# A ViT block with windowed attention and a top-2 expert layer: VectorE splits the first half, the second half's output product moves behind the first expert unit

## The reference

```python
h = tok(x)                      # patch embedding, layer norm, FFN, 8-head attention, FFN
h = layernorm(h + attn(h))      # one attention over the 64 tokens of an image
# ffn(h):
x = x + attention(rmsnorm(x)) @ wo.T            # 4 heads, causal
flat = rmsnorm(x) * ln2_w
probs = softmax(flat @ router_w.T)              # 8 experts
weights = top2(probs), divided by their sum
out = sum_e weights[:, e] * ((silu(flat @ w1[e].T) * (flat @ w3[e].T)) @ w2[e].T)
h = layernorm(h + x + out)
```

## Time and profile before

| | us |
|---|---|
| median of three runs (126.09 to 126.19) | 126.18 |
| the profiled execution | 125.92 |
| its span, first to last instruction | 124.1 |
| PE busy | 111.9 (90%) |
| DVE busy | 84.9 (68%) |
| ACT busy | 62.7 (50%) |
| POOL busy | 15.5 (12%) |

### The profile page before, as it was taken

How to read it: one execution, slowest core, us unless ns; L and a number is a source line. 1 busy time by engine, 2 the same in 40 slices (tenths; PEclk the granted TensorE clock), 3 DMA queues, 4 the chain that set the end, 5 groups by cost and what they waited for, 6 DMA issues and landing times.

```text
span 124.1 us, 2332 instructions
## 1 busy us (share of the span) xinstructions
PE 111.9 (90%) x904; PEld 75.4 (61%) x910; DVE 84.9 (68%) x183; ACT 62.7 (50%) x123; POOL 15.5 (12%) x42
## 2 busy tenths in 40 slices
PE   5998978899999889998699998899999999989950
PEld 2345637486777655775587895787888873325540
DVE  0003325797999496579797653489689978999951
ACT  4005367956323185654764638475475656245240
POOL 7400035000000000000022004090012230000000
PEclk9999999999999999999999999999999999999996
DMA  4999980000000000000000000000000000000003
GB/s 132 392 404 428 416 352 5 0 0 0 5 0 0 0 8 0 3 0 5 0 0 0 5 0 0 0 5 0 0 0 0 0 0 3 0 0 5 0 0 85
DMA packets 2682, 6.99 MB, mean 56 GB/s; under 512 B 1264, under 2 KB 1392, under 8 KB 2544
## 3 DMA queue, kind: packets, MB, share of 16 engines
q1 hardware_dynamic: 2128, 6.72, 13.9%
q10 hardware_dynamic: 544, 0.13, 0.5%
HBM read 6.59 MB, written 0.26 MB: 55 GB/s over the span
## 4 chain that ended last, share of the span: by engine, by line
PE 67%; DVE 19%; ACT 5%; issue 4%; POOL 2%; POOLq 1%; DVEq 0%; ACTq 0%
PE PS L650 7%; PE PS L651 7%; PE PS L292 4%; PE PS L317 3%; PE PS L533 3%; PE PS L327 3%; PE PS L658 3%; PE PS L284 3%; PE PS L519 3%; PE PS L381 3%; DVE top L1136 2%; DVE shifted L1138 2%; PE PS L391 2%; PE PS L667 2%; PE PS L356 2%
## 5 line engine op out<-in xcount | busy, mean ns | idle before, releaser
L650 PE MATMUL PS<-xf,up_hi 128*128 128x512 f32 x44 | 17.8, 404 | 0.0
L651 PE MATMUL PS<-xf,up_lo 128*128 128x512 f32 x44 | 17.4, 395 | 0.0
L1330 DVE TENSOR_TENSOR shared_h<-PS,shared_f 128x512 f32<-128x512 f32 x22 | 14.9, 683 | 3.2 <-ACT shared_f L921 2.7
L921 ACT ACTIVATE shared_f<-PS 128x512 f32<-128x512 f32 x22 | 13.0, 596 | 6.3 <-PE PS L651 6.3
L1136 DVE TENSOR_REDUCE top<-PS 128x8 f32<-128x512 f32 x12 | 8.3, 688 | 3.7 <-PE PS L356 1.8
L650 PEld LDWEIGHTS PS<-xf,up_hi 128*128 128x128 f32 x44 | 8.3, 188 | 2.1 <-DVE shared_h L1330 0.2
L749 ACT ACT_TABLE_LOAD x7 | 9.0, 1283 | 0.8 <-PEq L1537 0.7
L651 PEld LDWEIGHTS PS<-xf,up_lo 128*128 128x128 f32 x44 | 8.3, 188 | 1.8
L820 ACT ACTIVATE probs<-PS 128x512 f32<-128x512 f32 x8 | 4.8, 597 | 7.9 <-PE PS L367 7.8
L1138 DVE TENSOR_TENSOR shifted<-PS,top 128x512 f32<-128x512 f32 x12 | 8.3, 692 | 0.4
L1066 DVE TENSOR_REDUCE sq_sums<-squares 128x4 f32<-128x256 f32 x8 | 3.3, 418 | 7.3 <-ACT squares L772 4.2
(11 more groups left out here) (196 smaller groups left out, 213.8 us busy)
## 6 DMA issues: line engine op xcount, KB each, us to landing
shared_x<-x_dram SPq DMA_DIRECT2D x3, 576.0 KB, 4.6
shared_x<-x_dram SPq DMA_DIRECT2D x3, 512.0 KB, 7.8
up_w<-pack_d_dram SPq DMA_DIRECT2D x1, 1408.0 KB, 12.1
pack_c_sb<-pack_c_dram SPq DMA_DIRECT2D x1, 796.5 KB, 13.5
pack_b_sb<-pack_b_dram SPq DMA_DIRECT2D x1, 455.0 KB, 9.2
down_w<-pack_e_dram SPq DMA_DIRECT2D x1, 352.0 KB, 13.7
pack_a_sb<-pack_a_dram SPq DMA_DIRECT2D x1, 162.0 KB, 6.3
out_dram<-normed SPq DMA_DIRECT2D x2, 64.0 KB, 1.8
```

What stands on the lines that cost most here:

```text
L650: mm(up, up_hi[:, at:at + P], moving, start=True, stop=False)
L651: mm(up, up_lo[:, at:at + P], moving, start=False, stop=True).then_inc(sem("up_mm"), 1)
L921: f(gate[:, n % UPBUF, :], PS[:, UP_BANKS[n % UPBUF][0], :], ACT.Silu).then_inc(sem("gated"), 1)
L1330: v.tensor_tensor(hh[:, ch, :, g * HC:(g + 1) * HC], PS[:, UP_BANKS[n % UPBUF][1], :].rearrange("q (s c) -> q s c", s=2), gate[:, n % UPBU ...
```

## The change

`PARTS_AT` goes from 5 to 6 and `ROUTE_AT` from 6 to 7. The high part is made by VectorE and not by ScalarE, in both halves. For half 0 VectorE does high and low part ahead of the second half's `divide`, and TensorE turns the parts ahead of `mixed_to_features("att3", 7, 1)`. `output3(1)` goes from before unit 0 to between units 0 and 1, with `squares3(1)` behind ScalarE's first Silu. VectorE's `sum_squares("rms2", 1)` goes behind its product of unit 1, `normalised(1)` and `high_part(1)` behind unit 2, and `low_part(1)` and `residual(1)` behind unit 3. One more idle matmul is in `stay_awake`.

```diff
-        HIGH_AFTER = 1
-        PARTS_AT = 5
-        ROUTE_AT = 6
+        PARTS_AT = 6
+        ROUTE_AT = 7
...
 (TensorE)
-            stay_awake(2, 1)
+            stay_awake(3, 1)
+            parts_to_features(0)
             mixed_to_features("att3", 7, 1)
-            parts_to_features(0)
-            output3(1)
...
             for n in range(2 * CH):
                 g, ch = n // CH, n % CH
+                if n == 1:
+                    output3(1)
...
 (ScalarE)
-            def high_part(g):
-                act.wait_ge(sem("rms2_normed"), g + 1)
-                f(parts[:, 4 * g:4 * g + 4, 0, :].bitcast(F32R), tiles(h5n)[:, 4 * g:4 * g + 4], ACT.Copy)\
-                    .then_inc(sem("high_ready"), 1)
...
             bring_table(ACT.Silu)
-            high_part(0)
+            turned_copy(0)
             attended_copy3(1)
-            turned_copy(0)
-            squares3(1)
...
-                if n == HIGH_AFTER:
-                    high_part(1)
+                if n == 0:
+                    squares3(1)
...
 (VectorE)
+            def high_part(g):
+                ts = slice(4 * g, 4 * g + 4)
+                ve.wait_ge(sem("rms2_normed"), g + 1)
+                v.tensor_copy(parts[:, ts, 0, :].bitcast(F32R), tiles(h5n)[:, ts]).then_inc(sem("high_ready"), 1)
...
             normalised(0)
+            high_part(0)
+            low_part(0)
             divide("att3", 7, 1, FH, FHD)
-            low_part(0)
             turned_copy(0)
-            sum_squares("rms2", 1)
             residual(0)
...
-                if n == HIGH_AFTER - 1:
+                if n == 1:
+                    sum_squares("rms2", 1)
+                if n == 2:
                     normalised(1)
-                if n == HIGH_AFTER:
+                    high_part(1)
+                if n == 3:
                     low_part(1)
                     residual(1)
```

## The result

The changed kernel takes 128.69 us (median of four, 128.13 to 128.81) against 126.14 for the kernel before (126.04 to 126.19): a ratio of 1.0196, interval 1.017 to 1.0221. It is slower by 2.55 us; 129.1 was forecast, within 128.1 to 129.9. In experiment 1 the slower three of six executions are in the median but not in the ratio, which leaves out what lies more than 1.5% above a kernel's fastest execution; in every other kernel here nothing had to be left out.

What follows compares the result with a forecast made beforehand. TensorE, with 67% of the chain of waits, was taken as the bound in the units, VectorE after them. Parts of -0.42, +0.55, +1.73, +0.93, -0.06 and +0.24 summed to 2.97 us more: 129.1 us, range 128.1 to 129.9.

Steps and rivals of the forecast that it cites:

- Into unit 0: Ahead of unit 0: VectorE's 0.29 copy and earlier parts let unit 0 start at 79.36, 0.42 us gained.
- The output product behind unit 0: Between units 0 and 1: `output3(1)` adds 0.55 us, and `sum_squares(1)` starts at 82.86, before at 80.31.
- The copy beside the casts: Second half's high part on VectorE: one GpSimd cast holds it until 85.36; it ends at 85.65, `residual(1)` at 87.30.
- Rivals A and B: Second half's high part: A, casts don't hold the copy, 128.6, chance 0.17; B, both casts hold it, 129.7, chance 0.12.
- The group of transposes: TensorE behind unit 5: transposes load at 87.36 and unit 6 starts 0.55 us later, at 87.91.
- The router a unit later: Router's chain one unit later while `ROUTE_TURN` stays 20: TensorE waits some 1.3 at the turn; 0.93 us in the sum.
- The constant of 13.50: From the unit's start behind the router's products to `routes_to_rows`: 13.50 us, putting the turn at 103.23.
- Both stalls: TensorE waits 1.86 us ahead of the transposes and some 1.3 ahead of `routes_to_rows`, the second on top.
- Centring: After the units: second centring moves ahead of the first `weight_rest`, pushes VectorE by 0.33, of which 0.24 us is left.
- Rivals C and D: C: one stall only (transposes or turn), 127.3 or 127.8, chance 0.10; D: side chains keep up with TensorE, 125.6, chance 0.05.
- Rival E, the clock: In the units: TensorE's clock falls to 1.2 GHz for two units after the new stalls, 131.0, chance 0.06.

Runs made afterwards that it cites:

- experiment 1: Changed kernel with `PARTS_AT` back to 5 and `ROUTE_AT` back to 6: 130.59 us, ratio 1.0287 to the kernel before.
- experiment 3: Changed kernel with the second half's VectorE steps each one unit earlier: 127.42 us, ratio 1.0139 to the kernel before.
- experiment 4: GpSimd's casts `pick_rest` and `pick` put ahead of the second norm's roots: changed kernel 128.33 us, ratio 1.0192; kernel before, ratio 0.9981.
- experiment 2: Changed kernel with `PARTS_AT` 5, `ROUTE_AT` 6 and seven idle matmuls ahead of TensorE's wait for `residual(1)`: 128.34 us, ratio 1.0187 to the kernel before.
- experiment 5: Changed kernel with `routes_to_rows` ahead of unit 21 instead of 20: 127.59 us, ratio 1.0143 to the kernel before.
- experiment 6: Changed kernel with the residual's sums back behind units 17 and 18, centrings behind 19 and 20: 127.85 us, ratio 1.0161 to the kernel before.
- all four repairs: Changed kernel with second half's VectorE steps one unit earlier, GpSimd's casts early, sums and centrings at old units, `routes_to_rows` ahead of unit 21: 125.96 us, ratio 1.0011.

## Why the prediction was right, and where its sum was off

The mechanism came as forecast, in this order of steps:

- **Into unit 0.** Forecast at 2.49, measured 2.51. The 0.29 for the copy, estimated between rows of other operations, held exactly; its bounds were 0.28 and 0.42, so some luck is in that.
- **The output product behind unit 0.** `sum_squares(1)` forecast at 5.99, measured 5.89. Going from 3.44 to 5.89 is the root of the loss, and experiment 3 gives 1.07 of it back by one unit.
- **The copy beside the casts.** It was held by one cast: 0.43 (forecast 0.46). Rivals A and B, no cast and both, are out by experiment 4. The term that was mis-sized is the next: I had `pick` start only when the copy was done, at 0.91 behind T. It started 0.69 behind `normalised(1)`, as in the earlier trace rows, and only ran 1.10 instead of 1.04. So the low part, 0.65, was held for 0.24 and not for 0.39, and the residual ended at 10.15 and not at 10.43: 0.28 too much, 0.10 of it already in the place of `sum_squares`.
- **The group of transposes.** I gave it 0.55 before the next unit's load; after a pause it takes 0.39 (86.54 to 86.93). 0.16 too much. With this the turn is 2.29 later, not 2.73.
- **The router a unit later.** The distance from the router to the turn is 13.48 to 13.52 in every row of the table with the clock up but one (13.88, where the casts are early and unit 20 stands in front of the turn, so that TensorE itself is the late one). The constant of 13.50 was right, and so was the time made from it. But I booked 0.93 of the sum on the router's shift as a price on top of the stall, and this part of the mechanism was wrong: experiment 2 shows that there is no such price, and in experiment 1 the clock covered it. Both stalls are one chain, from `sum_squares(1)` over GpSimd's root, residual, transposes and router to the turn. Its unit numbers only say which of the two places TensorE waits at. What is free to move is the turn (experiment 5).
- **Centring.** Forecast 0.24; experiment 6 gives 0.48, of which 0.25 is the late start of unit 20's product, which I didn't foresee. It made up for about half of what the two errors above had put in, and that is luck: without it the trace would have shown 2.50 where 2.97 was forecast.
- **Rivals C and D.** Both stalls came, so C is out. D wanted the residual by 85.5, 8.6 behind `normalised(0)`, and the end 0.6 earlier than before. It also wanted the router's split by 100, 23.1 behind. With all four repairs the residual ends at 8.49, but the turn comes at 24.57 and the end at 44.35: the first condition is met, the second not, and no gain comes.
- **Rival E, the clock.** Not in this kernel: its pauses of TensorE are 1.39 and 1.09, and the mean clock of its five executions is 0.991 to 1.000. But it was nearer than its chance of 0.06 says: one unit more of pause, 2.34, brought the clock down in three of six executions for certain (mean 0.971 to 0.973), and by their times in two more (0.987).

In numbers: 2.97 forecast, less 0.28 and 0.16, plus 0.25, is 2.78; the trace has 2.75, and the medians are 2.55 apart.

## What to carry to other kernels

When a step is put behind other work in an engine's queue, follow the chain that starts at it to the next place where the bounding engine waits, and add the whole delay once; moving the middle of such a chain to another slot neither cost nor saved here, as long as the chain and not the slot was what came last. An engine that is hardly busy can still hold another one with work that nobody needs yet: put such work where the other does nothing. And where one engine is made to wait, look whether the work put between can be taken from what stands behind the wait: moving the turn by one constant was worth 0.93 us in the changed kernel and 0.45 in the kernel before with early casts, more than the 0.40 that the change gains ahead of unit 0.

## What the runs showed of the hardware

- GpSimd's 128x756 and 128x1024 casts hold VectorE's operations that read only SBUF: a two-input subtraction of 0.41 took 0.65 and 1.07, a one-input copy of 0.29 took 0.43; neither with the casts elsewhere. `normalised(1)`, which reads PSUM, took 0.43 beside `pick_rest` and 0.42 without it. The release came 0.13 to 0.15 before the cast's recorded end, and such ends of GpSimd are rough in the profile. By the Trainium skill ("SBUF — State Buffer", SBUF: two separate sides) the pair of ports is locked for an instruction; the runs agree that both kinds of operation are held. In the other direction they show less than a full block: `pick`, whose record starts 0.20 before the copy ends, ran 1.10 instead of 1.04 (1.10 with the copy alone moved, too).
- A pause of TensorE of 2.34 us was followed, 1.3 us after its end, by a granted clock of 0.50 to 0.53 for some 7 us in the profiled execution. The longest of the six executions took 3.1 us more than the one whose clock stayed up. Pauses of 1.39 and 1.09 in the changed kernel were not followed by a fall. Seven idle matmuls in the pause prevented it in five executions (mean clock 0.991 to 0.999).
- VectorE's product of unit 20 starts about 0.25 us late in the four kernels in which its predecessor is a sum (changed, one unit earlier, casts early, turn at 21), against the kernels in which it is a centring; unit 19's product behind a sum is not late. Not settled.
